# Gate weights spread by DMA and products shared between GpSimd and VectorE in a fused attention and expert kernel

## The reference

```
x = x + conv_attention(group_norm(x))          # softmax attention over 4096 points
t = tokens(x)                                  # 4 x 4096 tokens of 128 channels
t = t + scan_attention(layer_norm(t))          # 8 heads
t = t + experts(layer_norm(t))                 # 8 experts, the best 2 of each token

scan_attention:  k, v = silu(x @ W_kv); s = q . k
                 m = cummax(s); u = cumsum(exp(s - m)); w = cumsum(exp(s - m) * v); mean over heads of w / u
experts:         p = softmax(x @ router_w + b); top 2, renormalised
                 sum over the two of p * (x @ expert_w[e] + expert_b[e])
```

## Time and profile before

| quantity | value |
|---|---|
| median of three timed runs | 2835.81 us |
| profiled execution, its own time | 2831.05 us |
| its span (first to last instruction) | 2829.3 us |
| TensorE busy | 2642.4 us (93%) |
| VectorE busy | 2260.3 us (80%) |
| ScalarE busy | 1840.3 us (65%) |
| GpSimd busy | 1767.4 us (62%) |
| mean granted TensorE clock | 0.981 of full speed |

### The profile page before, as it was taken

How to read it: one execution, slowest core, us unless ns; L and a number is a source line. 1 busy time by engine, 2 the same in 40 slices (tenths; PEclk the granted TensorE clock), 3 DMA queues, 4 the chain that set the end, 5 groups by cost and what they waited for, 6 DMA issues and landing times. The chain is left out here.

```text
span 2829.3 us, 37348 instructions
## 1 busy us (share of the span) xinstructions
PE 2642.4 (93%) x11107; PEld 1901.2 (67%) x11107; DVE 2260.3 (80%) x3458; ACT 1840.3 (65%) x3367; POOL 1767.4 (62%) x1455
## 2 busy tenths in 40 slices
PE   6999999999999999999999999968799899899788
PEld 2888877788877788887788887734355455455334
DVE  4788887788887788887778888617888888898995
ACT  4667677666677667667766667757766666655540
POOL 3677777777776777776777777825544444444340
PEclk8999999999999999999999999989999999999999
DMA  1000000100000010000001001014332333223210
GB/s 63 5 12 8 12 12 8 38 9 16 8 8 12 8 42 8 12 12 8 8 12 34 8 11 43 16 50 165 124 120 105 116 112 117 106 71 131 98 71 26
DMA packets 48378, 130.76 MB, mean 46 GB/s; under 512 B 11472, under 2 KB 14096, under 8 KB 38960
## 3 DMA queue, kind: packets, MB, share of 16 engines
q1 hardware_dynamic: 48176, 128.39, 13.5%
HBM read 110.94 MB, written 17.43 MB: 45 GB/s over the span
## 5 line engine op out<-in xcount | busy, mean ns | idle before, releaser
L224 POOL TENSOR_TENSOR p_lo<-pf,p_hi 128x512 fp32r<-128x512 f32 x1024 | 1320.5, 1293 | 432.6 <-ACT p_hi L502 430.3
L497 ACT ACTIVATE pf<-s_ps 128x512 f32<-128x512 f32 x1024 | 612.9, 599 | 529.5 <-PE s_ps L376 528.3
L632 DVE TENSOR_REDUCE mx<-m_ps 128x1 f32<-128x512 f32 x1024 | 702.1, 687 | 302.6 <-PE m_ps L359 298.5
L648 DVE TENSOR_TENSOR sum_ps<-sum_ps,pf 128x512 f32<-128x512 f32 x960 | 661.1, 689 | 21.1 <-ACT pf L497 20.8
L502 ACT CAST p_hi<-pf 128x512 fp32r<-128x512 f32 x1024 | 627.5, 613 | 0.0
L1011 POOL TENSOR_TENSOR acc<-acc,ay 128x512 f32<-128x512 f32 x192 | 255.8, 1332 | 280.6 <-DVE ay L1326 280.1
L374 PE MATMUL s_ps<-q_hi,kd_hi 128*128 128x512 f32 x1024 | 427.2, 417 | 0.0
L359 PE MATMUL m_ps<-w_both,q_hi 128*128 128x512 f32 x1024 | 405.5, 398 | 12.1 <-DVE mx L632 6.2
L388 PE MATMUL om_ps<-p_hi,v_hi 128*128 128x512 f32 x1024 | 401.3, 392 | 4.7 <-POOL p_lo L224 4.7
L376 PE MATMUL s_ps<-q_lo,kd_hi 128*128 128x512 f32 x1024 | 399.6, 390 | 0.0
L375 PE MATMUL s_ps<-q_hi,kd_lo 128*128 128x512 f32 x1024 | 399.5, 390 | 0.0
(11 more groups left out here) (205 smaller groups left out, 3586.9 us busy)
## 6 DMA issues: line engine op xcount, KB each, us to landing
bq<-weight_rows SPq DMA_DIRECT2D x64, 1024.0 KB, 4.9
xb<-in_x_dram SPq DMA_DIRECT2D x8, 1024.0 KB, 6.4
rb_sb<-inverse_rows SPq DMA_DIRECT2D x32, 256.0 KB, 3.7
tokens<-xb SPq DMA_DIRECT2D x32, 256.0 KB, 2.0
tp<-tokens SPq DMA_DIRECT2D x32, 256.0 KB, 5.1
rb<-norm_rows SPq DMA_DIRECT2D x32, 256.0 KB, 4.1
tv<-tokens SPq DMA_DIRECT2D x32, 256.0 KB, 5.3
out_dram<-tv SPq DMA_DIRECT2D x32, 256.0 KB, 2.3
```

What stands on the lines that cost most here:

```text
L224: nc.gpsimd.tensor_tensor(p_lo[:, r, :], pf[:, r, :], p_hi[:, r, :].bitcast(F32), ALU.subtract).then_inc(lo_done, 1)
L497: nc.scalar.activation(pf[:, g % RING, :], s_ps[:, g % 2, :], ACT.Exp, scale=SCALE).then_inc(exp_done, 1)
L632: nc.vector.tensor_reduce(mx[:, n % 2, sub, chunk:chunk + 1], m_ps[:, j % 2, :], AX.X, ALU.max).then_inc(m_max, 1)
L648: nc.vector.tensor_tensor(sum_ps[:], sum_ps[:], p, ALU.add).then_inc(sum_done, 1)
```

## The change

The matmul `spread` and its two banks go away. ScalarE writes the turned gates twice, to `l_sb` in plain float32 and to `gt`. SyncE writes the rows of `l_sb` to DRAM (`gate_rows`, four DMAs in a group of four blocks) and reads them back spread over the partitions into a new tile `gb` of two halves, four experts each (`gate_spread`, two DMAs of 1 MB in a block). The products `gated` read `gb` instead of PSUM. In blocks 0 to 25 GpSimd makes six of the eight and VectorE makes experts 3 and 7; from block 26 (`FREE`) each makes four. Product `e` stands in slot `e + 3` (`G_LAG`), the expert matmul in slot `e + 5` (`X_LAG`), so that the last of them run in the next step. `xg` keeps its three buffers. The freed banks give `v_ps` a third and `mo_ps` a second bank. On GpSimd, `add_head(v, h)` moves one slot later; the softmax rows on VectorE and parts of `gates` move one slot earlier; `output` moves from the start of the step to slot 5; on SyncE `store` moves behind the weight DMAs. The diff below has the tiles first and then SyncE, GpSimd, TensorE, ScalarE and VectorE in that order.

```diff
-    V_LAG, F_LAG = 5, 11
+    V_LAG, F_LAG, G_LAG, X_LAG = 5, 11, 3, 5
+    FREE = NBLK - (F_LAG - V_LAG)
...
+        gb = sb("gate_b", [C, 2, HALF, TOK])
...
-        v_ps = psum("v_ps", [C, 2, BANK])
+        v_ps = psum("v_ps", [C, 3, BANK])
-        g_ps = psum("g_ps", [C, 2, BANK])
-        mo_ps = psum("mo_ps", [C, BANK])
+        mo_ps = psum("mo_ps", [C, 2, BANK])
...
+        def by_vector(f, e):
+            return e % 2 == 1 if f >= FREE else e % 4 == 3
...
+            def gate_rows(s):
+                sp.wait_ge(gr_act, s + 1)
+                for b in range(B):
+                    sp.dma_start(gates_d[s, b, :, :], l_sb[QUAD * b:QUAD * b + E, :]).then_inc(gr_out, 16)
+
+            def gate_spread(i, j):
+                s, b, cols = place(i)
+                sp.wait_ge(gr_out, 16 * B * (s + 1))
+                if i:
+                    sp.wait_ge(xg_pool, pool_gated(i - 1, HALF * (j + 1) - 1))
+                    after(sp, xg_dve, vector_gated(i - 1, HALF * (j + 1) - 1))
+                sp.dma_start(gb[:, j, :, :].rearrange("p e n -> p (e n)"),
+                             gates_d[s, b:b + 1, HALF * j:HALF * (j + 1), :].rearrange("o e n -> o (e n)")
+                             .to_broadcast([C, HALF * TOK])).then_inc(gb_in[j], 16)
...
                 k, v, f = j, j - V_LAG, j - F_LAG
-                if stage(f - 1):
-                    store(f - 1)
                 if stage(v + 1) and j % B != 0:
                     weight_spread(v + 1, 0)
...
                     norm_rows(j // B + 1)
                 if stage(k + 2):
                     norm_spread(k + 2)
+                if stage(f):
+                    gate_spread(f, 1)
                 if rows_at(j) is not None:
                     weight_rows(rows_at(j))
                 if stage(v + 1) and j % B == 0:
                     weight_spread(v + 1, 0)
                 if stage(v + 1):
                     weight_spread(v + 1, 1)
+                if stage(f - 1):
+                    store(f - 1)
+                if stage(f + 1):
+                    if (f + 1) % B == 0:
+                        gate_rows((f + 1) // B)
+                    gate_spread(f + 1, 0)
...
+            def gated(f, e):
+                pool.wait_ge(gb_in[e // HALF], 16 * (f + 1))
+                after(pool, x_pe, f * E + e - 2)
+                if e == 0:
+                    pool.wait_ge(t2_dve, f + 1)
+                nc.gpsimd.tensor_tensor(xg[:, (f * E + e) % 3, :], gb[:, e // HALF, e % HALF, :], tv[:, f % NV, :],
+                                        ALU.mult).then_inc(xg_pool, 1)
...
-            for j in range(STEPS):
-                k, v = j, j - V_LAG
+            nc.gpsimd.memset(g32[:], 0.0).then_inc(clr, 1)
+
+            for j in range(STEPS + 1):
+                k, v, f = j, j - V_LAG, j - F_LAG
                 for h in range(HEADS):
+                    if h == 0 and stage(v - 1):
+                        add_head(v - 1, HEADS - 1)
+                    if stage(f - 1) and h < G_LAG and not by_vector(f - 1, E + h - G_LAG):
+                        gated(f - 1, E + h - G_LAG)
+                    if stage(f) and h >= G_LAG and not by_vector(f, h - G_LAG):
+                        gated(f, h - G_LAG)
                     if stage(k + 1) and h == 1:
                         scaled(k + 1)
                     if stage(k + 1) and h == 5:
                         low(k + 1)
-                    if stage(v):
-                        add_head(v, h)
+                    if stage(v) and h:
+                        add_head(v, h - 1)
...
-                after(pe, y_dve, v * HEADS + h - 1)
-                project(v_ps[:, h % 2, :], h, 1, v).then_inc(v_pe, 1)
+                after(pe, y_dve, v * HEADS + h - 2)
+                project(value_bank(v, h), h, 1, v).then_inc(v_pe, 1)
...
-                pe.matmul(mo_ps[:], eb_lo[:, b, :], gt[:, s % 2, :], start=False, stop=False)
...
+                after(pe, out_dve, f - 1)
+                pe.wait_ge(gt_act, s + 1)
+                pe.matmul(mo_ps[:, f % 2, :], eb_hi[:, b, :], gt[:], start=True, stop=False)
+                pe.matmul(mo_ps[:, f % 2, :], eb_lo[:, b, :], gt[:], start=False, stop=False)
...
-                    if stage(f) and h == 0:
-                        spread(f, 0)
...
-                    if stage(f):
-                        if h == 0:
+                    if stage(f - 1) and h < X_LAG:
+                        expert(f - 1, E + h - X_LAG)
+                    if stage(f) and h >= X_LAG:
+                        if h == X_LAG:
                             expert_bias(f)
-                        expert(f, h)
-                    if norm2_at(j, 2) is not None and h == 7:
+                        expert(f, h - X_LAG)
...
-                nc.scalar.copy(gt[:, s % 2, :], st_ps[:]).then_inc(gt_act, 1)
+                act.wait_ge(lt_pe, s + 1)
+                nc.scalar.copy(l_sb[:], st_ps[:]).then_inc(gr_act, 1)
+                after(act, x_pe, (B * s - 1) * E + 1)
+                nc.scalar.copy(gt[:], st_ps[:]).then_inc(gt_act, 1)
...
                 v, f = j - V_LAG, j - F_LAG
-                if stage(f - 1):
-                    output(f - 1)
                 for h in range(HEADS):
+                    if stage(f - 1) and h < G_LAG and by_vector(f - 1, E + h - G_LAG):
+                        gated(f - 1, E + h - G_LAG)
+                    if stage(f) and h >= G_LAG and by_vector(f, h - G_LAG):
+                        gated(f, h - G_LAG)
+                    if stage(f - 1) and h == X_LAG:
+                        output(f - 1)
                     if stage(v):
                         weigh(v, h)
-                    if stage(f):
-                        if h == 0:
-                            gated(f, 0)
-                        if h + 1 < E:
-                            gated(f, h + 1)
                     if stage(v):
                         scan(v, h)
                     if rows_at(j) is not None:
                         s = rows_at(j)
                         if h == 0:
                             maxima(s)
-                        if h == 1:
                             shifted(s)
                         if h == 3:
                             sums(s)
+                            inverse(s)
                         if h == 4:
-                            inverse(s)
-                        if h == 5:
                             new_weights(s)
                     if norm1_at(j, 1) is not None and h == 1:
                         variance(norm1_at(j, 1))
```

More of the change, by code:

```diff
@@ L876, in scan_attention_and_experts @@
             sem(n) for n in ("var2_dve", "msq2_act", "ln2_act", "rst2_act", "gate", "th_act"))
-        gt_pe, gt_act, g_pe, xg_dve, x_pe, out_dve = (
-            sem(n) for n in ("gt_pe", "gt_act", "g_pe", "xg_dve", "x_pe", "out_dve"))
+        gt_pe, gt_act, gr_act, gr_out, xg_pool, xg_dve, x_pe, out_dve = (
+            sem(n) for n in ("gt_pe", "gt_act", "gr_act", "gr_out", "xg_pool", "xg_dve", "x_pe", "out_dve"))
+        gb_in = [sem(f"gb_in{i}") for i in range(2)]
+        clr = sem("clr")
         block = ctx.enter_context(nc.Block())
@@ L1115, in row_sums @@
                     mm.then_inc(s_pe, 1)
[L1117 to L1123, removed]
             def expert_bias(f):
                 s, b, cols = place(f)
-                after(pe, out_dve, f)
-                pe.matmul(mo_ps[:], eb_hi[:, b, :], gt[:, s % 2, :], start=True, stop=False)
-                pe.matmul(mo_ps[:], eb_lo[:, b, :], gt[:, s % 2, :], start=False, stop=False)
+                after(pe, out_dve, f - 1)
+                pe.wait_ge(gt_act, s + 1)
+                pe.matmul(mo_ps[:, f % 2, :], eb_hi[:, b, :], gt[:], start=True, stop=False)
+                pe.matmul(mo_ps[:, f % 2, :], eb_lo[:, b, :], gt[:], start=False, stop=False)
             def expert(f, e):
-                pe.wait_ge(xg_dve, f * E + e + 1)
-                pe.matmul(mo_ps[:], ew[:, e, :], xg[:, e % 3, :], start=False, stop=(e == E - 1)).then_inc(x_pe, 1)
-            for j in range(STEPS):
+                if by_vector(f, e):
+                    pe.wait_ge(xg_dve, vector_gated(f, e))
+                else:
+                    pe.wait_ge(xg_pool, pool_gated(f, e))
+                pe.matmul(mo_ps[:, f % 2, :], ew[:, e, :], xg[:, (f * E + e) % 3, :], start=False, stop=(e == E - 1)).then_inc(x_pe, 1)
+            for j in range(STEPS + 1):
                 k, v, f = j, j - V_LAG, j - F_LAG
                 for h in range(HEADS):
-                    if stage(f) and h == 0:
-                        spread(f, 0)
                     if stage(v):
                         value(v, h)
-                    if stage(f) and h + 1 < E:
-                        spread(f, h + 1)
                     if stage(k - 1) and h == 0:
@@ L1157, in _ @@
                         turn_logits(norm2_at(j, 1))
-                    if stage(f):
-                        if h == 0:
+                    if stage(f - 1) and h < X_LAG:
```

(26 more changed lines are left out.)

31 lines of the change are left out of this document (18 added, 13 removed).

## The result

The changed kernel takes 2736.03 us (median of four runs, 2734.94 to 2740.3) against 2835.32 us in the same session: ratio 0.9658, interval 0.964 to 0.9676. That is 99 us less. 2766 was forecast, with a range from 2730 to 2808.

What follows compares the result with a forecast made beforehand. No single engine bounds all steps: TensorE the plain one, VectorE the softmax-row one. Gains of 52 (full steps), 13 (steps without keys), 2.5 (tail) and 2.5 us (attention-only) sum to 70, giving 2766 us, range 2730 to 2808.

Steps and rivals of the forecast that it cites:

- rival C: Third bank swallows table-load and `bq` waits, products meet an idle GpSimd: 31 us more gain, 2735; chance 0.13.
- two terms beneath it: VectorE, per step: +1.2 us port waits for two products and `residual`, +1.0 us longer distance from `weigh` to `scan`.
- port wait: VectorE instructions with two SBUF inputs wait for GpSimd's: 0.5 us for each product, 0.2 for `residual`.
- The plain step at 21.8 us: Fourth kind of full step, bounded by TensorE: 23.62 us less 1.84 for eight `spread` matmuls.
- cost and free nothing: Doubling the output banks on TensorE was given no effect, since `output` has a whole step now.
- the 8.2 us of waits: TensorE's waits before expert matmuls for late products in four steps; most should go with experts two slots behind.
- Rival A: Port exclusion is dear, 1.3 us instead of 0.5 for each VectorE product: about 30 us less gain, 2796; chance 0.12.
- Rival B: Gate rows arrive late or push `bq` in the shared DMA queue: 25 to 40 us less gain, about 2798; chance 0.12.
- the wait for `bq`: VectorE's 2.4 us wait in four steps; the forecast left it in place, in the second kind of step.
- the stop behind the table loads: In the third kind of step `weigh` waits 2.27 us behind ScalarE's table loads; the forecast kept this stop.
- Rival D: GpSimd becomes the bound; a round trip of product, add, scan, `value` and expert matmul closes: slower, 2855; chance 0.06.
- the forecast's own terms: Tail: 9.1 us a block instead of 10.4, transpose 5 us sooner, gate-row trip costs 9; stated as -2.5 us.

Runs made afterwards that it cites:

- the PSUM experiment: Kernel with two value banks, VectorE's products reading a constant PSUM bank of zeros instead of gate rows in SBUF: 2754.92 us, ratio 0.9723.
- the two-bank kernel: The changed kernel with two value banks instead of three, the third left unused: 2769.11 us, ratio 0.9777.

## Why the prediction was right, and where it was not

The direction and the wide range held. The forecast's own range, 2745 to 2785, did not: 2736 is the number of rival C, whose working did not come, so that the match with 2735 is luck. By stretch, forecast against measured gain: full steps 52 and 68.4 us, attention-only steps 2.5 and 8.9, steps 32 to 35 10.6 and 14.4, step 36 and the tail 5 and 5.5. TensorE's slot lost 0.23 us as forecast.

VectorE's busy time fell by the 1.4 us a step that were forecast in steps 16 to 19, and by 1.7 over all full steps. That the first number fits is in part luck too: two terms beneath it were off by some 0.4 us and cancelled. A product took 1.31 us in the mean in steps 16 to 19, so 0.63 of port wait instead of 0.5, and `residual` went from 0.85 to 1.17; but without a product behind it `weigh` took only 0.6 us a step more of VectorE's busy time, not 1.0 (the rest is idle time). The Trainium skill's rule of an exclusive shared pair of ports ("SBUF — State Buffer", section "SBUF: two separate sides", not the section that the prediction names) agrees with these lengths and with the PSUM experiment: 0.68 us with one SBUF input, 1.14 with two.

The term that was mis-sized is the third value bank. The prediction gave it 2.5 us in the attention-only steps and nothing in the full ones; taking it away costs 33 us, 8.8 of them in the attention-only steps and 24.9 in the full ones. Without the bank the forecast is a gain of 67.5 us and the two-bank kernel measured 64. The plain step at 21.8 us was worked out from one in which TensorE seemed to have no gap. It had none in the record, but it was a step of a two-bank kernel: with a bank more TensorE comes to that step with a lead, and part of the step's work is already done.

The second wrong step is that twice the output banks "cost and free nothing". In the new order, where the bias matmul would meet `output` in the same slot, the second bank saves 78 us. It does not explain the forecast's error: the kernel before did not pay this price, and the forecast was made for the new order with both banks.

The lag of the experts was credited with the 8.2 us of waits in four steps, 43 us in 21 steps at the most. The waits went, but not by the second slot of lag alone: with the old lag of one slot 12.3 and 1.5 us of them are left in 400 us, and the time is 17 us longer. Taking single parts back costs 78 (GpSimd's products), 33 (value bank), 23 (rows earlier) and 17 us (second slot of lag), and the `spread` is worth 24 in the two-bank kernel. These do not add up to a division of the 99 us, since each was measured with the others in place. No lag (135) and one output bank in the new order (78) are states that neither kernel was in.

Rival A did not come: the time was below the forecast though the port wait of a product was above it, and the exclusion costs 14 us at most in the two-bank kernel. Rival B did not: without the spreads the full steps are the same. Rival C came in part: the wait for `bq` went, for which both the third bank (1.6 us are left with two) and the earlier rows (1.3 with the old slots) are needed; the stop behind the table loads did not go (3.83 us), and the products did not meet an idle GpSimd. Rival D did not come: GpSimd is busy for 98% of the plain step, more than the 85 to 95% forecast, and still TensorE never waits for its products in the full steps. Its round trip appears only when the lag is taken away.

In the tail the forecast's own terms give 4 x 1.3 + 5 - 9 = 1.2 us, not 2.5. A block takes 8.6 us where 9.1 were forecast and 10.4 were measured before; from the last `residual` to the last gate transpose it is 20.9 us (2667.27 to 2688.21) instead of 22.5, not 5 less; and the first product comes 8.3 us behind the transpose (2696.50), where 9 were forecast. From the last `residual` to the last `output` (2731.45) this is 64.2 us, as before (64.1). What was gained from step 36 on was gained in step 36, which went from 25.9 to 20.4 us.

## What to carry to other kernels

Between engines with queues of fixed order, put at least one slot between an instruction and the one on another engine that needs it: here the first slot was worth 118 us and the second 17. Where a new order makes an instruction wait for one of the same slot, as the bias would for `output`, a second bank pays, since a single such wait takes away the lead that the other buffers make. Read a step without gaps with care: the plain step's TensorE had none and still lost 2.7 us to one more bank. And when a part of a change is taken back for a test, set it to what the kernel before had; a state that neither kernel was in has a price, but not one that explains the gain.

## What the runs showed of the hardware

The port wait goes by instruction: a VectorE product with one SBUF input took 0.68 us in the mean of 45 cases from 2100 to 2660 us (the longest 0.69), with two 1.14 us in the mean (the longest 1.79), and GpSimd's products 1.32 us instead of 1.29 beside them. The DMA queue moved 324 GB/s over a whole step of 26.9 us, at 0.82 busy, and leaving the spreads out made the full steps no shorter (510.8 us against 510.5). 1 MB spreads of `bq` took 5.8 us to land in the median instead of 5.0.
